# Packing the experts' slots: 71 groups of 256, each group's weights gathered by its expert

## The reference

```python
logits = xf @ router_w.T                       # xf: 8192 tokens x 256
probs = softmax(logits); k_probs, k_idx = top_k(probs, 2)
capacity = int(1.25 * N * K / E) + 1           # 2561 for N 8192, K 2, E 8
rank = position of a (token, choice) among those of its expert
keep = rank < capacity
buf[expert, rank] = xf[token]                  # where kept
h = silu(einsum('ech,ehf->ecf', buf, w1))      # w1: 8 x 256 x 1024
out_buf = einsum('ecf,efh->ech', h, w2)        # w2: 8 x 1024 x 256
combined[token] = sum over its 2 choices of out_buf * gate
return combined + x
```

## Time and profile before

| | us |
|---|---|
| median of 3 runs (lowest, highest) | 4143.76 (4142.36, 4148.31) |
| the profiled execution's own time | 4151.12 |
| its span | 4149.4 |
| mean granted TensorE clock | 0.971 |
| experts stage, first DMA to the first work of combine | 2885.6 to 3907.8 |

### The profile page before, as it was taken

How to read it: one execution, slowest core, us unless ns; L and a number is a source line. 1 busy time by engine, 2 the same in 40 slices (tenths; PEclk the granted TensorE clock), 3 DMA queues, 4 the chain that set the end, 5 groups by cost and what they waited for, 6 DMA issues and landing times. The chain is left out here.

```text
span 4149.4 us, 77109 instructions
## 1 busy us (share of the span) xinstructions
PE 3908.8 (94%) x24340; PEld 2523.2 (61%) x24340; DVE 3238.0 (78%) x4396; ACT 2417.5 (58%) x3574; POOL 760.9 (18%) x662
## 2 busy tenths in 40 slices
PE   6965999999999999999999999996999999999897
PEld 5643444444444444444444444442999999999897
DVE  5545999999999999999999999995546455454587
ACT  3434877778878877887887887874122222212233
POOL 1103333330000000000000000000333323333387
PEclk8977999999999999999999999998999999999999
DMA  6743445544444444444444444432312122121497
GB/s 231 278 187 103 121 127 132 126 116 145 126 120 141 126 121 140 126 121 140 126 121 140 126 123 138 126 102 63 96 44 81 44 64 60 44 74 44 154 322 259
DMA packets 411579, 526.74 MB, mean 127 GB/s; under 512 B 175956, under 2 KB 307230, under 8 KB 393598
## 3 DMA queue, kind: packets, MB, share of 16 engines
q1 hardware_dynamic: 343070, 457.63, 36.3%
q0 software_dynamic: 58112, 46.82, 4.2%
q10 hardware_dynamic: 10336, 21.52, 1.7%
HBM read 332.15 MB, written 124.42 MB: 110 GB/s over the span
## 5 line engine op out<-in xcount | busy, mean ns | idle before, releaser
L816 ACT ACTIVATE at_ex<-at_st 128x1024 f32<-128x1024 f32 x1024 | 1046.9, 1023 | 127.5 <-PE at_st L941 105.8
L954 PE MATMUL at_pv<-at_ex,at_v 128*64 128x512 f32 x4096 | 991.5, 605 | 0.0
L696 DVE TENSOR_REDUCE at_mx<-at_fr 128x1 f32<-128x512 f32 x1024 | 702.7, 686 | 139.0 <-PE at_fr L961 83.1
L839 ACT ACTIVATE at_fr<-at_fr 128x512 f32<-128x512 f32 x1024 | 599.6, 586 | 343.6 <-PE at_fr L964 289.4
L1279 ACT ACTIVATE ex_hs<-ex_h 128x366 f32<-128x366 f32 x448 | 214.0, 478 | 791.6 <-PE ex_h L1325 479.1
L707 DVE TENSOR_TENSOR at_sum<-at_sum,at_ex 128x1024 f32<-128x1024 f32 x512 | 624.6, 1220 | 12.8 <-ACT at_ex L816 1.7
L954 PEld LDWEIGHTS at_pv<-at_ex,at_v 128*64 128x64 f32 x4096 | 248.4, 136 | 508.5 <-issue 493.2
L1338 PE MATMUL ex_o<-ex_w,ex_hT 128*122 128x256 f32 x4032 | 498.6, 283 | 19.7 <-DVE ex_hT L1221 18.7
L1338 PEld LDWEIGHTS ex_o<-ex_w,ex_hT 128*122 128x122 f32 x4032 | 483.8, 184 | 25.9 <-DVE ex_hT L1221 24.2
L1179 POOL COPY ex_idx<-ex_slots 122x3 int32 (+1 forms) x56 | 33.2, 593 | 2514.6 <-DMA ex_slots<-scr_table 1962.8
L964 PE MATMUL at_fr<-at_kfar,at_qh 64*128 64x512 f32 x1024 | 467.4, 456 | 17.3 <-DVE at_mx L696 6.5
(11 more groups left out here) (141 smaller groups left out, 5125.7 us busy)
## 6 DMA issues: line engine op xcount, KB each, us to landing
at_cq<-scr_c SPq DMA_DIRECT2D x62, 1024.0 KB
at_ck<-scr_c SPq DMA_DIRECT2D x62, 1024.0 KB
scr_v<-pj_v SPq DMA_DIRECT2D x64, 512.0 KB, 4.6
at_v<-scr_v SPq DMA_DIRECT2D x64, 512.0 KB
at_swpq<-at_rawq SPq DMA_DIRECT2D x128, 256.0 KB
at_swpk<-at_rawk SPq DMA_DIRECT2D x128, 256.0 KB
at_rec<-scr_rec SPq DMA_DIRECT2D x256, 128.0 KB
scr_o<-at_oT SPq DMA_DIRECT2D x64, 512.0 KB
```

The source lines that it names most:

```text
L696: e.reduce_max(mx[k // QB][:, h * QB + k % QB:h * QB + k % QB + 1], fr[h][:, :], AX.X).then_inc(s_tr[h], 1)
L816: e.activation(ex[k][:, :, :], st[u % 2][:, :, :], ACT.Exp, scale=SCALE).then_inc(s_exp, 1)
L839: e.activation(fr[h][:, :], fr[h][:, :], ACT.Relu).then_inc(s_pos[h], 1)
L954: mm = e.matmul(pv[n][rows[h], :], v[i.u][:, kt, rows[h]], ex[kt][:, h, :], start=(kt == 0), stop=(kt == KT - 1))
```

## The change

Slots are packed. An expert gets as many groups of 256 slots as its kept rows need, one expert behind the other, and 71 groups (the most that can be needed) are computed. The expert of a group is known only on the chip, so its weights are fetched by an indirect DMA with row numbers made by the route (`keep["widx"]`: expert * 128 + partition), and split for every group. w1 and w2 lie in HBM as 8 x 128 rows of 2048 values (8 KB), each row what one partition holds.

```diff
-SLOT_P = 122  SLOT_T = 21  CAPP = SLOT_P * SLOT_T  PART_T = 3 ...
+GT = 2
+GP = GT * P
+GROUPS = (NTOK * 2 + NE * (GP - 1)) // GP
-NSLOT = NE * CAPP
+NSLOT = GROUPS * GP
 # route, DVE, behind the running sum
+            then(e.tensor_scalar(need[:, :], cum[:, :, NT - 1], float(CAP), float(GP - 1), ALU.min, ALU.add))
+            floor(need, need, GP)                      # 2 operations
+            then(e.tensor_scalar(need[:, :], need[:, :], -WHOLE, float(GP), ALU.add, ALU.mult))
+            then(e.tensor_tensor_scan(end[:, :], ones[:, 0:NE], need[:, :], 0.0, ALU.mult, ALU.add))
+            then(e.tensor_tensor(out=base[:, :], in0=end[:, :], in1=need[:, :], op=ALU.subtract))
+            then(e.tensor_tensor(out=past[:, :, :], ... op=ALU.is_ge))     # 71 x 7
+            then(e.tensor_reduce(out=who[:, :], in_=past[:, :, :], axis=AX.X, op=ALU.add))
+            then(e.tensor_scalar(keep["widx"][:, :], who[:, :], float(P), part[:, 0:1], ALU.mult, ALU.add))
 # route, for each of the two choices
-                then(e.tensor_tensor(out=over[:, :], in0=over[:, :], in1=rk[:, :], op=ALU.add))
+                then(e.tensor_tensor(out=row[:, :], in0=rk[:, :], in1=pos[:, :], op=ALU.add))
+                floor(blk_of, row, P)
+                then(e.tensor_scalar(blk_of[:, :], blk_of[:, :], -WHOLE, float(1 - NSLOT), ALU.add, ALU.mult))
+                then(e.scalar_tensor_tensor(out=row[:, :], ...))
 # experts, POOL, written out for all groups
+            for g in range(GROUPS):
+                q = g % 2
+                if g >= 2:
+                    e.wait_ge(s_w1l, 2 * (g - 1))
+                weights(g, io["w1"], raw1[q], s_w1[q])
+                if g == 0:
+                    e.wait_ge(s_slots, 16)
+                if g >= 2:
+                    e.wait_ge(s_tr, g - 1)
+                for c in range(GT):
+                    e.indirect_dma_start(out=xg[q][:, c, :], ...)
+                if g >= 2:
+                    e.wait_ge(s_w2l, 2 * (g - 1))
+                weights(g, io["w2"], raw2[q], s_w2[q])
 # experts, DVE, group a (one = the next group)
+                outputs(a.next(-1))
+                low1(one, 0)
+                for j in range(NQ):
+                    hidden(a, j)                       # 128x512, low half only
+                turned(one)
+                low1(one, 1)
+                low2(one, 0)
+                low2(one, 1)                           # low1, low2: 128x1024 each
 # experts, ACT
+            def silu(a, j):
+                fs = slice(2 * j, 2 * j + 2)
+                e.wait_ge(s_h, a.n(NQ, j + 1))
+                wait(e, s_hT, a.n(NQ, j + 1 - NQ))
+                if j == 0:
+                    wait(e, s_o, a.n(1, -1))
+                e.activation(hT[a.u][:, 0, fs, :]..., phid[:, j, :], ACT.Silu).then_inc(s_silu, 1)
+                e.activation(hs[:, fs, :]..., phid[:, j, :], ACT.Silu).then_inc(s_silu, 1)
+                high1(one, 0)
+                for j in range(NQ):
+                    silu(a, j)
+                high1(one, 1)
+                high2(one, 0)
+                high2(one, 1)                          # copies 128x1024 into float32r
 # experts, PE
+                hidden(a)      # 48 matmuls, weights 128x128, 256 columns, 4 banks of PSUM
+                turn(a.next(1))
+                down(a)        # 48 matmuls, weights 128x128, 256 columns
```

More of the change, by code:

```diff
@@ L1133, in experts_phase @@
-        s_g = [sem(f"g{q}") for q in range(2)]
-        s_os = [sem(f"os{q}") for q in range(2)]
-        s_split = [sem(f"split{q}") for q in range(2)]
-        s_apart = sem("apart")
-        s_slots, s_idx, s_tr, s_xh, s_xT, s_h, s_silu, s_hh, s_hT, s_o, s_oe = (
-            sem(n) for n in ("slots", "idx", "tr", "xh", "xT", "h", "silu", "hh", "hT", "o", "oe"))
+        stage, wo = seam["stage"], seam["wo"]
+        raw1 = [stage[q][:, 0:W] for q in range(2)]
+        raw2 = [stage[q][:, W:] for q in range(2)]
@@ L1150, in _, with store @@
[L1150 to L1155, removed]
-                    load(pr * 2 + q, q)
-            e.wait_ge(s_split[0], NE // 2 * 4)
-            e.dma_start(raw[0][:, :].rearrange("p (r s) -> p r s", r=HP),
+            e.dma_start(slots[:, :], scr["table"].rearrange("(p n) o -> p (n o)", p=P)).then_inc(s_slots, 16)
+            def store(a):
+                e.wait_ge(s_oe, a.n(1, 1))
+                e.dma_start(scr["eo"].rearrange("(g c p) d -> g p c d", c=GT, p=P)[a.n(), :, :, :], out[a.u][:, :, :]).then_inc(s_os[a.u], 16)
@@ new lines, in outputs, with body @@
+            def outputs(a):
+                e.wait_ge(s_os[a.u], a.same(16, 16))
+                e.wait_ge(s_o, a.n(1, 1))
+                e.tensor_copy(out[a.u][:, :, :], po[:, :, 0:D]).then_inc(s_oe, 1)
+            def body(a, first=False):
+                one = a.next(1)
+                if not first:
+                    outputs(a.next(-1))
[6 more added lines that the diff above has]
+                low2(one, 1)
@@ new lines, in _ @@
+            low1(At(0, 0), 0)
+            turned(At(0, 0))
+            low1(At(0, 0), 1)
+            low2(At(0, 0), 0)
+            low2(At(0, 0), 1)
+            groups(e, lambda a: body(a, isinstance(a.base, int) and a.off == 0))
+            body(At(0, GROUPS - 2))
+            last = At(0, GROUPS - 1)
+            outputs(last.next(-1))
+            e.wait_ge(s_wh, 1)
+            e.tensor_tensor(out=wo[1][:, :, :], in0=wraw, in1=wo[0][:, :, :].bitcast(F32), op=ALU.subtract).then_inc(s_wl, 1)
@@ new lines, in hidden @@
+                e.wait_ge(s_xT, a.n(1, 1))
+                for j in range(NQ):
+                    if j % 2 == 0:
+                        e.wait_ge(s_w1l, a.n(2, j // 2 + 1))
+                    wait(e, s_silu, a.n(2 * NQ, 2 * j + 2 - 2 * NQ))
+                    for f in (2 * j, 2 * j + 1):
+                        for ws, xs in PASSES:
+                            for k in range(KD):
+                                mm = e.matmul(phid[:, j, f % 2 * GP:(f % 2 + 1) * GP], w1[q][:, ws, f, k, :], xT[q][:, xs, k, :],
+                                              start=(ws + xs + k == 0), stop=(ws == 1 and k == KD - 1))
+                    mm.then_inc(s_h, 1)
@@ L1603, in build @@
             "read": sb("read", [P, NT, 2], I32),
+            "widx": sb("widx", [P, GROUPS], I32),
         }
```

331 lines of the change are left out of this document (138 added, 193 removed).

## The result

The changed kernel took 3949.65 us (median of 4 runs, 3945.9 to 3955.35) against 4143.06 (4 runs, 4136.33 to 4148.31): ratio 0.9535, 95% interval 0.9517 to 0.9554. The forecast was 3995 with a range of 3975 to 4080.

A forecast was written before the change was run, and what follows sets the result against it. TensorE's matmuls were taken to bound the experts stage. Matmul span -145.9, earlier start -7.9 and route +4.8 make -149.0 us: profiled 4151.1 becomes 4002.1, and the median, 7.4 lower, gives 3995, range 3975 to 4080.

The forecast's parts named there:

- Rival 1: Experts stage: engine chains, the port or a late landing make a group 13.0 to 13.5 us, 4070 to 4105; chance 0.22.
- rival 2: Weight gathers: GpSimd's price goes by bytes, 7.6 us each, 18.3 us a group, +451 us, 4446; chance 0.09.
- Rival 4: Experts stage: packing doesn't reduce the work; dismissed because the 71 groups are fixed in the code; no chance given.
- The place with 0.2 us to spare: Within a group, the last pair of hidden values is ready at 8.1 us and PE needs it at 8.3.
- The port: Experts stage: gathers stand still during DVE's two-operand SBUF reads; four fit a group. An exclusive lock would mean 13.5 us.
- Route: Route stage: added small DVE operations in series and one small load, +4.8 us (bounds 3.5 and 7).
- seams: Kernel before, changes of expert pair: DVE's weight splits delay two parts in each of three places, 18 us in all.
- so I take 120: Experts matmuls: 120 ns a step as in combine, 96 x 0.120 in a group of 11.95 us, 848.5 us for 71.
- Rival 3: Experts stage: matmuls go by the 109 ns pace, 74 us less, 3921; chance 0.03.
- The matmuls at another pace: Sign that the prediction is wrong: expert matmuls not starting 120 ns apart in the trace after.
- nothing beside it: Route stage: the change there costs +4.8 us of small operations and a load, and no more.
- The start: Experts stage: first layer starts 13.5 us into the stage, 7.9 us less than before (bounds 0 and 12).

## Why the prediction was wrong

Right:
- **What bounds it.** PE by its matmuls, before and after. PE's idle time after is 2 us; without the weights' work nothing changes, with 78% more traffic nothing either. Rival 1 (chains, port, landing) and rival 2 (gathers by bytes) did not occur: the weight gathers took 0.94 to 1.69 us where 1.0 to 1.7 was taken, and landed in 5.7 to 9.3 us, with no wait of PE for one after the start. Rival 4 neither.
- **The place with 0.2 us to spare** held even with PE faster, so there was more to spare; ACT and DVE were 0.4 us a group quicker than costed.
- **The port.** The prediction weighed the Trainium skill, SBUF — State Buffer, section "SBUF: two separate sides", whose exclusive lock would have made gathers stop DVE (13.5 us a group). The measurement decides against that price here: DVE took 9.1 us a group beside four gathers, and the six of the run with two more made no group slower. DVE's 142 subtractions of 128x1024 for the first layer's weights took 1.21 to 1.23 us each, those that began during a gather too. It is the gather that takes longer, as the prediction read from combine: of the 142 weight gathers 69 took 1.34 to 1.69 us, nearly all the while beside subtractions back to back, and 73 took 0.94 to 1.0:

```profile
3210.27 2.35 DVE L1238 TENSOR_TENSOR ex_w<-seam_stage,ex_w 128x1024 fp32r<-128x1024 f32 x2
3210.62 1.68 POOL L1211 DMA_INDIRECT seam_stage<-in_w,keep_widx  x1 [5.94 <-DVE ex_w L1234]
...
3215.48 0.97 POOL L1211 DMA_INDIRECT seam_stage<-in_w,keep_widx  x1 [0.31 <-issue]
```

- **Route** +4.8, **seams** 18 (19.2 measured), DVE and ACT per group within 0.5 us, traffic 220 GB/s (228 measured); POOL's 6.5 us was 1.6 too high.

Wrong, by term of the sum:
- **"so I take 120": the pace of a step, 28 us of the miss.** The term 96 x 0.120 was read from combine's row, as of the same shape. The shape is the same, but combine's tiles lie a multiple of 256 bytes apart and the experts' 64 off that, where a step takes 113.4 or 117.8 ns. Where the distance is 0 mod 256, the prediction's own model holds to 2 us: it gives 1022.3 - 153.8 = 868.5 us for the experts stage, and the three such runs took 866.8 to 867.9. Rival 3 had the right sign and far too large a size (109 ns, 74 us, chance 0.03). Its condition, "Only a different layout of the weights speaks for it", came near the cause, but the prediction did not ask how the layout differs from combine's. "The matmuls at another pace" was also its own sign of being wrong, and that sign came. The Trainium skill, TensorE: Matmul & The Clock Gate, section "Wait — 56ns, not 53.3ns?", would have 109.2 ns; no distance tried came to it, 113.4 is the nearest.
- **"nothing beside it": the table, 17.7 us in the profiled pair.** The change also moved every word that the route's scatters write, into a stage whose code doesn't change, and the prediction costed that edit only as small operations in the route. The kernel before with the table alone changed gained 25 us (17 to 32) by its times, so over the medians this may be more than 17.7.
- **The start** was 3.3 us earlier than estimated and **the end** 2.5 later ("stays at 4.3"): the last rows are now one store of 256 KB, issued 0.83 us after the last matmul, and combine follows 6.0 us after that. What in those 6 us is longer wasn't tried.
- The 8.8 us in the projections are scatter between executions, and 1.2 us are combine's.

27.9 + 17.7 + 8.8 + 3.3 - 2.5 + 1.2 = 56.4, against the 56.2 between -205.2 and -149.0. Of these 56, 11 are of the profiled pair alone, which lies further apart than the medians; the forecast missed by 45. The range failed for the same reason: its lower end (3975) allowed for a pace of 119 to 121 ns, the spread of two rows, and nothing for the stages that the diff doesn't touch. The pace decided it: the three kernels at 0 mod 256, with the same gain in the attention, took 3979 to 3982 us, inside the range.

Still open: why one program runs in turns of two groups in some executions and at 117.8 ns throughout in others (five executions at a distance of 64 went the one way, four the other); and what inside PE or SBUF makes the distance count. That it is distance and not place was tested on the experts' tiles with the weights fixed; there both moved together only once. Combine's tiles bear it out at distance 0: they begin 128, 160, 192 and 224 bytes past a multiple of 256 in the kernels before and after, with all tiles 32 on, and with ten more groups, and in each the median step is 120 ns (means 119.8 to 119.9).

## What to carry to other kernels

A pace read from another stage's row holds for its shape and for how its tiles lie; before using it to 4%, look at the distance between the loaded and the moving tile mod 256 bytes, and keep it off 0 where PE is the bound. A tile's size is part of a change, even a table of 568 bytes that no matmul reads. When an edit moves the words that small scatters write, price it in the stage in which the scatters run, not only where the indices are made.

## What the runs showed of the hardware

- Matmuls of float32r, 128x128 loaded and 256 columns moving, a load each, at clock 1.00: 120.0 ns a step with tiles 0 mod 256 bytes apart, 118.6 at 128, 117.5 / 120.0 at 160, 116.8 / 118.5 at 32, and 113.4 or 117.8 at 64.
- Indirect scatters of 128 single words, two at a time: 5.1 to 5.8 us of waiting per pair where neighbours in rank are adjacent words, 2.9 to 3.1 where they are 84 or 568 bytes apart, with the attention's transfers landing later beside the former (loads of v 9.3 against 6.8 us).
- An indirect gather of 128 rows of 8 KB holds POOL for 0.94 to 1.69 us, as one of 1 KB rows does (0.95 to 1.63), and 406 GB/s were held with no group slower.
- VectorE's subtractions of 128x1024 took 1.21 to 1.23 us with and without a gather beside them; gathers beside two of them back to back took up to 1.69 us, others 0.95.
